# Moving 29 of 99 destination gathers from the dense stage to the scores stage, and the XD stores behind step 61

## What is computed

```python
h = relu(layernorm(x)); x = x + L0(h, node_type, src, dst, edge_type)   # typed attention
h = relu(layernorm(x)); x = x + L1(h, src, dst)                         # gated differences
h = relu(layernorm(x)); x = x + L2(h, edge_index)                       # sum of neighbours, MLP
h = relu(layernorm(x)); x = x + L3(h, src, dst)                         # attention with heads
```

```python
k, q, v = typed_matmul(h, k_lin), typed_matmul(h, q_lin), typed_matmul(h, v_lin)
t_edge = einsum('nd,rde->rne', q, rel_att)[etype, dst]
logits = sum(t_edge * k[src]) * (rel_pri / 8)[etype]
```

## Time and profile before

| | |
|---|---|
| runs, median (lowest to highest) | 6195.22 us (6193.31 to 6201.44) |
| profiled execution | 6195.52 us |
| its span, first to last instruction | 6193.7 us |
| PE, DVE, ACT, POOL busy, whole span | 81%, 73%, 40%, 62% |
| dense stage | 166 to 1400 us |
| scatters L748 on POOL | 396, first 167.1, last 767.3 us, median 973 ns |
| gathers L758 on POOL | 396, first 770.2, last 1363.9 us, median 999 ns |
| scores: gathers L832 on POOL | 396, first 1401.0, last 2376.1 us, median 999 ns |

### The profile page before, as it was taken

The page is one execution under the profiler, slowest core; times in us unless marked ns, Lnnn a source line. Parts: engine busy times, 40 slices in busy tenths (PEclk is TensorE's granted clock), DMA queues, the critical chain, the costliest instruction groups (busy, mean ns, idle before and its releaser), DMA issues. The chain is left out here.

```text
span 6193.7 us, 73617 instructions
## 1 busy us (share of the span) xinstructions
PE 5013.1 (81%) x19049; PEld 2686.4 (43%) x19049; DVE 4517.1 (73%) x7949; ACT 2488.5 (40%) x7048; POOL 3864.5 (62%) x3983
## 2 busy tenths in 40 slices
PE   0899489988999996999978886666688877878886
PEld 0455245544555553566644443222233334444443
DVE  4788377767888886999966665666688766666666
ACT  0788367763333332455533332222233333333333
POOL 1777787764444441000058887888788857777787
PEclk9999688889999998999965555555688866777666
DMA  9333145543333332999943333444566622222221
GB/s 357 109 105 105 34 134 136 136 119 80 81 80 79 81 80 46 277 286 285 285 108 83 83 83 79 115 114 114 121 164 165 156 75 66 65 65 64 63 59 41
DMA packets 868574, 739.52 MB, mean 119 GB/s; under 512 B 568092, under 2 KB 575218, under 8 KB 868032
## 3 DMA queue, kind: packets, MB, share of 16 engines
q1 hardware_dynamic: 566112, 525.53, 29.8%
q0 software_dynamic: 102464, 90.84, 8.1%
q10 hardware_dynamic: 199584, 118.45, 6.3%
HBM read 461.89 MB, written 276.55 MB: 119 GB/s over the span
## 5 line engine op out<-in xcount | busy, mean ns | idle before, releaser
L1298 POOL DMA_INDIRECT df_hs<-u,keep_idx x396 | 510.0, 1288 | 829.4 <-POOLq L209 709.1
L832 POOL DMA_INDIRECT sc_xg<-t,keep_gather x396 | 466.2, 1177 | 546.1 <-DVE sc_h L194 413.8
L748 POOL DMA_INDIRECT t<-keep_ptr_pay,keep_scat_ptr x396 | 472.1, 1192 | 253.4 <-issue 128.8
L1298 POOL DMA_INDIRECT hd_gat<-u,keep_idx x396 | 487.2, 1230 | 157.0 <-issue 115.2
L758 POOL DMA_INDIRECT den_xd<-t,keep_gather x396 | 474.3, 1198 | 122.3 <-issue 115.8
L1831 POOL DMA_INDIRECT out_x<-hd_x,keep_scat_out x396 | 451.0, 1139 | 146.7 <-issue 119.1
L1298 POOL DMA_INDIRECT pr_gat<-sd,keep_idxsd x396 | 411.8, 1040 | 88.8 <-issue 70.8
L1298 POOL DMA_INDIRECT ml_gat<-u,keep_idx x396 | 401.1, 1013 | 98.6 <-issue 70.3
L629 ACT ACTIVATE den_dh<-den_den_dn_cent,den_den_dn_rstd 128x64 f32<-128x64 f32 x1584 | 397.8, 335 | 4.8 <-DVE den_den_dn_rstd L609 0.5
L1287 PE MATMUL at_ps_m<-at_vx,keep_msg_twice 128*128 128x512 f32 x792 | 364.2, 603 | 24.4 <-DVE at_vx L1178 24.4
L981 PE MATMUL sc_ps_r<-sc_qx,keep_weights 128*64 128x512 f32 x792 | 361.1, 598 | 1.0 <-DVE sc_prod L896 1.0
(11 more groups left out here) (297 smaller groups left out, 13083.3 us busy)
## 6 DMA issues: line engine op xcount, KB each, us to landing
u<-den_dh SPq DMA_DIRECT2D x198, 256.0 KB
t<-tab_row ACTq DMA_DIRECT2D x99, 272.0 KB, 11.3
tab_x<-in_x SPq DMA_DIRECT2D x99, 256.0 KB
den_dx<-in_x SPq DMA_DIRECT2D x99, 256.0 KB
out_x<-den_dx SPq DMA_DIRECT2D x99, 256.0 KB
sc_et<-in_etype_row SPq DMA_DIRECT2D x99, 256.0 KB
at_v<-vt SPq DMA_DIRECT2D x198, 128.0 KB, 5.4
at_et<-in_etype_row SPq DMA_DIRECT2D x99, 256.0 KB
```

Source lines behind the costliest of these rows:

```text
L748: pool.indirect_dma_start(pairs, bass.IndirectOffsetOnAxis(ap=e.scat_ptr[:, c:c + 1], axis=0), e.ptr_pay[:, c, :], None, bounds_check=NP * ...
L832: pool.indirect_dma_start(xg[i][:, u, :], None, e.T0, bass.IndirectOffsetOnAxis(ap=e.gather0[:, b.n, u:u + 1], axis=0), bounds_check=NP - ...
L1298: pool.indirect_dma_start(gat[i][:, u, :], None, table, bass.IndirectOffsetOnAxis(ap=idx_all[:, c:c + 1], axis=0), bounds_check=rows - 1, ...
```

## The change

Three constants and lists are new: 70 of the edge groups are early, 29 late, spread evenly (3, 6, 10, 13, ..., 98). In `dense` the scatters no longer wait for VectorE's steps; the gathers, of the 70 early groups only, follow them without such waits either, into 6 slots instead of 3; and SP's stores of them begin behind `den.sync(61)` and are spread over steps 61 to 98. In `scores` GpSimd gathers the destination rows of a late group itself, behind its source gathers, straight into the slot, and SP stores them to `XD` from there one step later; SP's load from `XD` is done for early groups only. The diff, cut:

```diff
+EARLY = 70
+LATE = [b for b in range(NG) if b * (NG - EARLY) // NG != (b + 1) * (NG - EARLY) // NG]
@@ dense
+        XU = 6
+        early = [b for b in range(NG) if b not in LATE]
+        xd = [s.sb(f"xd{i}", [P, TU, TW]) for i in range(XU)]
+        head = count * 61 // 99
+        def stored_at(n):
+            m, of = n - head, count - head
+            return range(len(early) * m // of, len(early) * (m + 1) // of) if 0 <= m < of else range(0)
@@ dense, gpsimd
-                half = count // 2
-                for n in range(half):
-                    wait(pool, den.x2_done, n, e.pool_passed)
-                    for c in range(CH * n // half, CH * (n + 1) // half):
-                        pool.indirect_dma_start(pairs, ...).then_inc(ptr_out, 16)
+                for c in range(CH):
+                    pool.indirect_dma_start(pairs, ...).then_inc(ptr_out, 16)
                 wait(pool, ptr_out, 16 * CH, e.pool_passed)
-                for n in range(half, count):
-                    wait(pool, den.x2_done, n, e.pool_passed)
-                    for b in edge_groups(n):
-                        i = b % U
-                        wait(pool, xd_out[i], 16 * (b // U), e.pool_passed)
+                for k, b in enumerate(early):
+                    i = k % XU
+                    wait(pool, xd_out[i], 16 * (k // XU), e.pool_passed)
@@ dense, sync
                     den.sync(sp, den.step(n))
-                    for b in edge_groups(n - 1):
-                        wait(sp, gathered[b % U], 16 * TU * (b // U + 1), e.sp_passed)
+                    for k in stored_at(n):
+                        i = k % XU
+                        wait(sp, gathered[i], 16 * TU * (k // XU + 1), e.sp_passed)
+                        sp.dma_start(edge_rows(e.XD, early[k] * GE, TW), xd[i][:, :, :]).then_inc(xd_out[i], 16)
@@ scores, gpsimd, behind the source gathers of group b.n
+                    if b.n in LATE:
+                        wait(pool, type_kept, b.n - (U - 1), e.pool_passed)
+                        wait(pool, xd_out[i], 16 * (late_of(b.n) - 1), e.pool_passed)
+                        for u in range(TU):
+                            pool.indirect_dma_start(xg[i][:, TU + u, :], None, e.T0, ...).then_inc(dst_in[i], 16)
@@ scores, sync
-                        wait(sp, h_done, st.n - (U - 1), e.sp_passed)
-                        wait(sp, type_kept, st.n - (U - 1), e.sp_passed)
-                        sp.dma_start(xg[st.s][:, TU:R, :], edge_rows(e.XD, st.n * GE, TW)).then_inc(xd_in[st.s], 16)
+                        if st.n not in LATE:
+                            wait(sp, h_done, st.n - (U - 1), e.sp_passed)
+                            wait(sp, type_kept, st.n - (U - 1), e.sp_passed)
+                            wait(sp, xd_out[st.s], 16 * late_of(st.n), e.sp_passed)
+                            sp.dma_start(xg[st.s][:, TU:R, :], edge_rows(e.XD, st.n * GE, TW)).then_inc(xd_in[st.s], 16)
                     b = st.back(1)
+                    if b.on() and b.n in LATE:
+                        wait(sp, dst_in[b.s], 16 * TU * late_of(b.n), e.sp_passed)
+                        sp.dma_start(edge_rows(e.XD, b.n * GE, TW), xg[b.s][:, TU:R, :]).then_inc(xd_out[b.s], 16)
@@ scores, vector
                         v.wait_ge(gathered[st.s], 16 * TU * (st.k + 1))
-                        v.wait_ge(xd_in[st.s], 16 * (st.k + 1))
+                        if st.n in LATE:
+                            v.wait_ge(dst_in[st.s], 16 * TU * late_of(st.n))
+                        else:
+                            v.wait_ge(xd_in[st.s], 16 * early_of(st.n))
```

More of the change, by code:

```diff
@@ L731, in dense @@
         ptr_out = s.sem("ptr_out")
[L732 to L738, removed]
+        XU = 6
+        early = [b for b in range(NG) if b not in LATE]
+        xd = [s.sb(f"xd{i}", [P, TU, TW]) for i in range(XU)]
+        gathered, xd_out = s.sems("g", XU), s.sems("xdo", XU)
+        head = count * 61 // 99
+        def stored_at(n):
+            m, of = n - head, count - head
+            return range(len(early) * m // of, len(early) * (m + 1) // of) if 0 <= m < of else range(0)
         with nc.Block() as block:
@@ L743, in _ @@
                 pairs = e.T0.rearrange("n (a b) -> (n a) b", b=2)
-                half = count // 2
-                for n in range(half):
-                    wait(pool, den.x2_done, n, e.pool_passed)
-                    for c in range(CH * n // half, CH * (n + 1) // half):
-                        pool.indirect_dma_start(pairs, bass.IndirectOffsetOnAxis(ap=e.scat_ptr[:, c:c + 1], axis=0),
-                                                e.ptr_pay[:, c, :], None, bounds_check=NP * TW // 2 - 1,
-                                                oob_is_err=False).then_inc(ptr_out, 16)
-                wait(pool, ptr_out, 16 * CH, e.pool_passed)
-                for n in range(half, count):
-                    wait(pool, den.x2_done, n, e.pool_passed)
-                    for b in edge_groups(n):
-                        i = b % U
-                        wait(pool, xd_out[i], 16 * (b // U), e.pool_passed)
[L757 to L760, removed]
+                for c in range(CH):
+                    pool.indirect_dma_start(pairs, bass.IndirectOffsetOnAxis(ap=e.scat_ptr[:, c:c + 1], axis=0),
+                                            e.ptr_pay[:, c, :], None, bounds_check=NP * TW // 2 - 1,
+                                            oob_is_err=False).then_inc(ptr_out, 16)
+                wait(pool, ptr_out, 16 * CH, e.pool_passed)
+                for k, b in enumerate(early):
+                    i = k % XU
+                    wait(pool, xd_out[i], 16 * (k // XU), e.pool_passed)
+                    for u in range(TU):
+                        pool.indirect_dma_start(xd[i][:, u, :], None, e.T0,
+                                                bass.IndirectOffsetOnAxis(ap=e.gather0[:, b, TU + u:TU + u + 1], axis=0),
+                                                bounds_check=NP - 1, oob_is_err=False).then_inc(gathered[i], 16)
             @block.sync
@@ L765, in _ @@
                     den.sync(sp, den.step(n))
-                    for b in edge_groups(n - 1):
-                        wait(sp, gathered[b % U], 16 * TU * (b // U + 1), e.sp_passed)
-                        sp.dma_start(edge_rows(e.XD, b * GE, TW), xd[b % U][:, :, :]).then_inc(xd_out[b % U], 16)
+                    for k in stored_at(n):
+                        i = k % XU
+                        wait(sp, gathered[i], 16 * TU * (k // XU + 1), e.sp_passed)
+                        sp.dma_start(edge_rows(e.XD, early[k] * GE, TW), xd[i][:, :, :]).then_inc(xd_out[i], 16)
                 den.sync_end(sp)
-                for i in range(U):
-                    wait(sp, xd_out[i], 16 * (NG // U), e.sp_passed)
+                for i in range(XU):
+                    wait(sp, xd_out[i], 16 * len(range(i, len(early), XU)), e.sp_passed)
             @block.vector
@@ L816, in scores @@
         gathered, et_in, h_out, xd_in, v_out = [s.sems(n) for n in ("g", "et", "ho", "xd", "vo")]
+        dst_in, xd_out = s.sems("di"), s.sems("xdo")
+        early_of = lambda n: len([b for b in range(n % U, n + 1, U) if b not in LATE])
+        late_of = lambda n: len([b for b in range(n % U, n + 1, U) if b in LATE])
         l_turned, rows_kept, l_out = s.sem("lt"), s.sem("rk"), s.sem("lo")
@@ L834, in body @@
                                                 bounds_check=NP - 1, oob_is_err=False).then_inc(gathered[i], 16)
+                    if b.n in LATE:
+                        wait(pool, type_kept, b.n - (U - 1), e.pool_passed)
+                        wait(pool, xd_out[i], 16 * (late_of(b.n) - 1), e.pool_passed)
+                        for u in range(TU):
+                            pool.indirect_dma_start(xg[i][:, TU + u, :], None, e.T0,
+                                                    bass.IndirectOffsetOnAxis(ap=e.gather0[:, b.n, TU + u:TU + u + 1], axis=0),
+                                                    bounds_check=NP - 1, oob_is_err=False).then_inc(dst_in[i], 16)
                 run_groups(pool, body, U, 0)
@@ L863, in _ @@
                         wait(sp, sems[i], 16 * (NG // U), e.sp_passed)
+                for i in range(U):
+                    wait(sp, xd_out[i], 16 * late_of(NG - U + i), e.sp_passed)
             @block.vector
```

## The result

The changed kernel takes **6058.25 us** (median of 4 runs, 6054.13 to 6069.86) against 6194.53 of the kernel before: ratio 0.9781, 95% interval 0.9764 to 0.9798, 136.3 us less. The forecast was 6056. The profiled execution has a span of 6057.4 us, 136.3 under the 6193.7 of before. In two later sessions the kernel before itself took 6506 and 6607 us, and in the first of them the changed kernel was 3.1% slower than it; that belongs to the result too.

A forecast was written before the change was run, and what follows sets the result against it. Dense was taken as bound by GpSimd's gathers after a stall, scores by PE. +15 scatters, -174 gathers not made, +8 slower gathers, +11 at the end give -140; with +1 for scores 6056, range 6038 to 6078 (0.78).

The forecast's parts named there:

- The pace of the scatters at nothing: Dense: taking out the scatters' waits for VectorE gives 0.
- the pace never bound: Dense: before the scatters GpSimd waited only 0.3 us for VectorE, once.
- Scatters beside a busy VectorE: Dense: without the stall scatters take 1.556 us each and end at 783.5, +15 us; first gather at 785.4.
- The stall and SP's order: Dense: the 97.8 us stall goes; SP waits 13 us at step 61, costing about 1 us.
- The gathers: Dense after step 61: 1.53 us a gather, 11.3 us a step, still bound by GpSimd; last x load at 1203.6.
- The tail: Dense's end, last x load to first load of scores: 56.8 us is kept, so scores starts at 1260.4.
- Scores: 29 late groups stay hidden, 11.7 us of gathers in a 21.8 us window: +1 us, bounds 0 to +10.
- B: Rival, scores: GpSimd's added gathers hold up VectorE, 70 us lost, time 6126; chance 0.06.
- D: Rival, scores: late groups' second four gathers aren't hidden, 174 us against 140 won, time 6230; chance 0.04.
- E: Rival, scores: late groups late by a little, 10 to 55 us given back, 6067 to 6112; chance 0.06.
- The sum: Whole kernel: scores starts 139.9 us earlier, +1 us for scores, 6195.5 to 6056.6.
- (C): Rival, dense: it runs free at 10.25 us a step to the end, time 6002; chance 0.04.

The follow-up runs named there:

- E4: Changed kernel with the scatters' pace put back and 3 slots in dense instead of 6: 6063.12 us, ratio 0.9783 to the kernel before.
- E8: Changed kernel unaltered, run in a slow session where the kernel before takes 6505.92 us: 6717.65 us, ratio 1.0314.
- E11: Changed kernel with only the scatters' pace put back (6 slots stay), in a second slow session: 6571.24 us, ratio 0.9941 to the kernel before.
- E1: Changed kernel with EARLY = 99, so against the kernel before in effect only the stores move: 6205.25 us, ratio 1.0011.
- E2: Changed kernel with dense's old order (paced scatters, 3 slots, stores from step 50), only 29 groups moved to scores: 6118.26 us, ratio 0.9872.
- E3: Changed kernel with EARLY = 60, so 39 late groups: 6032.06 us, ratio 0.9734 to the kernel before.
- E10: Changed kernel with 66 early groups, no late one among scores' first six, stores over steps 63 to 103, paced scatters: 6008.1 us, ratio 0.9714.
- E12: The version of E10 once more, against the kernel before: 6018.93 us, ratio 0.9704.
- E9: The kernel before, unaltered, profiled on a third chip in a session like the first: 6205.21 us in one run.

## Why the prediction was right, and where not

*The pace of the scatters at nothing.* Right where it was predicted (0.3 us of waits; E4 within the interval), and not a property of the kernel: in the slow sessions the changed kernel is 3.1% slower without the pace (E8) and 0.6% faster with it (E11, 0.1 to 1.1%), each against the kernel before of its session. The step that failed there is "the pace never bound": the trace of one good session can't show more.

*Scatters beside a busy VectorE.* Forecast end of scatters 783.5, first gather 785.4; measured first gather 790.2. The rate was (787.31 - 167.3) / 395 = 1.570 us, not 1.556. It cost 4.8 us, and the end of the last scatter, 788.3, lies outside the 780 to 786 that were to show the forecast right.

*The stall and SP's order.* The stall went, as said, and the next wait was at step 61: 18.1 us, forecast 13. VectorE felt 6.7 us of it, not 1.

*The gathers.* 280 at (1215.64 - 790.22) / 279 = 1.525 us, forecast 1.53; a step 11.35 us, forecast 11.3. Dense did stay bound by GpSimd. The last x load left at 1207.16, forecast 1203.6. E1 and E2 fit the model from the other sides, each within 5 us of its stage times.

*The tail.* The term that was mis-sized: 62.9 us, not 56.8. A part of it is how far SP's x load runs ahead of VectorE at the end. It was used 3.5 us after its issue before and 4.0 after, but 14.1 in E2 and 14.9 in E3, with tails of 68.7 and 69.5. Less this lead the tail is 53.3 us before, 54.6 in E2 and E3, and 59.0 in the changed kernel. The rest goes with PE's granted clock over these us: 0.70 to 0.72 where it is 53 to 55 (before, E2, E3, E4, E10, E12), and 0.66 to 0.68 where it is more: 56.1 in E1, 57.5 in E9, 59.0 here. E9 is the kernel before, unaltered, so some 4 us of this tail differ from execution to execution and aren't the change's. Why the clock was lower isn't shown.

*Scores.* +1 us forecast, +0.1 measured: rivals B, D and E didn't come about. It began at 1270.1, past the 1253 to 1268 named as its sign. The window came out at 21.8 us, as worked out, the eight gathers at 11.5 for 11.7. VectorE's L157 in scores has 678/684/692 ns, so nothing of the hold-up of (B) either. By SBUF — State Buffer in the Trainium skill ("Who interferes with whom") it is the order of issue that decides whether VectorE or GpSimd is blocked at their shared ports. The trace agrees with one half of that only: gathers stretch beside VectorE (1.36 and 1.61 us above), VectorE's row doesn't. That a late group can cost at the start was named as the bound, +10, and E3 shows it at +4.

*The sum.* -130.3 at the start of scores where -139.9 was forecast: 9.6 us too good, 4.8 from the scatters, 6.1 from the tail, -1.2 from the gathers (rounded). The 6.1 us that the later stages gave weren't forecast at all and aren't the change's: their code is the same, and over all profiled runs outside the slow sessions they last between 3753.8 (E10) and 3768.4 us (E12). So the number was nearer than its terms were: the start of scores was missed by 9.6 us, and that the whole came out 2.6 us from the forecast in the profiled execution (-136.3 for -139.9 + 1) is in part luck.

(C), dense at its own pace, didn't happen with 70 groups but is what E10 reaches with 66 by giving GpSimd the tail's five steps.

## What to carry to other kernels

A long stall in one place says where a wait is paid, not what it costs: count the bounding engine's instructions from its start to its end (here 396 and 396 on GpSimd), and check by moving the stall away whether its time goes with it (E1: it doesn't) before crediting it to an edit. A wait that the trace of one session shows as free can bind in another (0.3 and 147.5 us here); leave it in if it costs nothing (E10 has it and is the fastest), and time a change in more than one session. If two traces of nearly the same code differ by a few us in a place that the edit doesn't touch, read the granted clock there, and a second execution, before giving them to the edit. When work is handed to a stage with room to spare, keep it out of the first few steps, where nothing has a lead yet.

## What the runs showed of the hardware

In one slow session, scatters issued back to back (0.97 us and 0.30 between) all but stopped the four other engines, though DMA was 5% busy (E8): 4 steps in 497 us, 47 us of VectorE work in 527, 94 of PE. Outside the slow sessions the same 396 scatters left dense's step at 10.25 us. In the slow one the rest of the kernel was slower too (scores 1046 for 1032 us, later stages 3846 for 3756 in the changed kernel). From one indirect DMA to the next GpSimd takes 1.27 to 1.30 us where nothing stretches it (1.33 in the mean of E8's 396 scatters), and 1.53 to 1.57 beside a VectorE that is busy 78 to 87% of the time. In the tail of dense, less SP's lead, PE's granted clock differs between two executions of one kernel (0.72 in the kernel before, 0.66 in E9), and the time with it (53.3 and 57.5 us).
